# Squares of the last four weight tiles taken in the first step, and the weights' lower parts by VectorE

## What is computed

```python
def attn(x):                                   # x already layer-normed
    kv_latent = x @ W_to_kv.T                  # 128
    c = kv_latent @ W_compress.T               # 64
    ch = layernorm(c) * ln_gamma + ln_beta
    q = rope(ch @ W_q_comp.T); k, v = split(ch @ W_kv_comp.T); k = rope(k)
    o = softmax(causal(q @ k.T / 8)) @ v
    z = o @ W_comp2lat.T
    return z @ W_to_kv + z @ W_out_res.T + b_out_res

def ffn(x):                                    # x already layer-normed
    hidden = silu(x @ W1.T) * (x @ W3.T)       # 2048
    return fwht(hidden) @ W2.T

x = x + attn(layernorm(x))
x = x + ffn(layernorm(x))
```

## Time and profile before

| | us |
|---|---|
| three runs | 2194.49, 2202.16, 2198.07 |
| median | 2198.07 |
| profiled execution | 2193.52 |
| its span, first to last instruction | 2191.7 |
| TensorE busy in the span | 2106.2 |
| VectorE, ScalarE, GpSimd busy | 1435.8, 941.5, 231.3 |
| mean granted TensorE clock | 0.988 |

### The profile page before, as it was taken

The page is one execution under the profiler, slowest core; times in us unless marked ns, Lnnn a source line. Parts: engine busy times, 40 slices in busy tenths (PEclk is TensorE's granted clock), DMA queues, the critical chain, the costliest instruction groups (busy, mean ns, idle before and its releaser), DMA issues. The chain is left out here.

```text
span 2191.7 us, 27021 instructions
## 1 busy us (share of the span) xinstructions
PE 2106.2 (96%) x9884; PEld 986.1 (45%) x9884; DVE 1435.8 (66%) x2758; ACT 941.5 (43%) x1437; POOL 231.3 (11%) x212
## 2 busy tenths in 40 slices
PE   6668999999999999999999999999999999999999
PEld 3433444444444444444444444444444444444444
DVE  7887676766667666765767666775757657663333
ACT  6846555434433534435444444435344444432221
POOL 2354554000000000000000000000000000000000
PEclk8889999999999999999999999999999999999999
DMA  8435324733337333544146333463236432363121
GB/s 326 152 115 198 126 78 132 192 105 132 103 104 176 100 107 111 142 146 140 57 130 167 119 117 106 120 169 120 80 111 167 132 124 75 113 149 119 69 80 75
DMA packets 231141, 278.65 MB, mean 127 GB/s; under 512 B 178016, under 2 KB 178144, under 8 KB 225632
## 3 DMA queue, kind: packets, MB, share of 16 engines
q1 hardware_dynamic: 231008, 276.91, 41.0%
HBM read 194.81 MB, written 39.85 MB: 107 GB/s over the span
## 5 line engine op out<-in xcount | busy, mean ns | idle before, releaser
L845 PE MATMUL PF<-XF,WS 128*128 128x512 f16 x1792 | 683.9, 382 | 16.0 <-DVE PF L1805 11.9
L846 PE MATMUL PF<-XF,WS 128*128 128x512 f16 x1792 | 681.6, 380 | 0.0
L847 PE MATMUL PF<-XF,WS 128*128 128x512 f16 x1792 | 681.3, 380 | 0.0
L869 PE MATMUL PD<-W2S,H 128*128 128x512 f16 x1024 | 388.1, 379 | 0.0
L870 PE MATMUL PD<-W2S,H 128*128 128x512 f16 x1024 | 388.1, 379 | 0.0
L871 PE MATMUL PD<-W2S,H 128*128 128x512 f16 x1024 | 388.1, 379 | 0.0
L1212 ACT ACTIVATE SH<-PF,afs 128x512 f32<-128x512 f32 x256 | 175.9, 687 | 405.6 <-PE PF L847 401.1
L845 PEld LDWEIGHTS PF<-XF,WS 128*128 128x128 f16 x1792 | 175.4, 98 | 254.3 <-issue 37.4
L1827 DVE TENSOR_TENSOR H<-SH,H 128x1024 f16<-128x1024 f32 x128 | 158.9, 1241 | 181.2 <-ACT H L1223 180.9
L847 PEld LDWEIGHTS PF<-XF,WS 128*128 128x128 f16 x1792 | 175.9, 98 | 213.0 <-issue 2.8
L1819 DVE SCALAR_TENSOR_TENSOR SH<-PF,afs,SH 128x512 f32<-128x512 f32 x256 | 191.6, 748 | 117.9 <-ACT SH L1212 105.3
(11 more groups left out here) (317 smaller groups left out, 2086.9 us busy)
## 6 DMA issues: line engine op xcount, KB each, us to landing
WS<-wscr SPq DMA_DIRECT2D x112, 896.0 KB, 4.9
W2S<-w2scr SPq DMA_DIRECT2D x30, 1024.0 KB, 6.5
ring<-x SPq DMA_DIRECT2D x56, 256.0 KB, 7.1
wscr<-WS SPq DMA_DIRECT2D x16, 896.0 KB, 4.0
out<-ring SPq DMA_DIRECT2D x56, 256.0 KB, 2.6
XF<-w SPq DMA_DIRECT2D x16, 512.0 KB, 7.8
RAW<-w13t SPq DMA_DIRECT2D x16, 512.0 KB, 4.0
xraw<-xT SPq DMA_DIRECT2D x28, 256.0 KB, 5.0
```

What stands on the lines that cost most here:

```text
L845: pe.matmul(bank, wh, th, start=i < 2 and j == 0, stop=False, skip_group_check=True)
L846: pe.matmul(bank, wh, tl, start=False, stop=False, skip_group_check=True)
L847: m = pe.matmul(bank, wl, th, start=False, stop=j == 1, skip_group_check=True)
L869: pe.matmul(PD[:, t % 2, :], th, wh, start=j == 0, stop=False)
```

## The change

Two things are changed in step 0 and ahead of it; from step 1 on the lists are the same.

1. The sums of squares of tiles 12 to 15 leave the hand-written part. Their rows are no longer loaded to XF but to the last eight places of the ring (`norm_row`), where the rows of x for chunks 2 and 3 come later; `norm_rows` of these four waits for what R and wsm are last read by, and `load_x` of chunks 2 and 3 waits for all 32 sums instead. ScalarE takes 12, 13 and 14 in tile 0, after the second silu, and 15 in tile 1, ahead of `copy_p5`. `tokens_high(0, i)`, which overwrites XF, waits for 24 sums.
2. All lower parts are VectorE's: `forms_low(h, part)`, part 0 for forms 0 to 3 and part 1 for forms 4 to 6, both counted by v_wl; GpSimd's `forms_low` and g_wl are gone. In a tile, part 0 stands after `fill(k, 2)`, behind `sum_c`, and part 1 behind `sum_e`; before, VectorE's stood ahead of `sum_c`.

With these go moves: `forms_high(h + 1, ...)` from before `fill(k, 0)` and after `copy_p5` to after `fill(k, 1)`; `forms(h + 2)` from j = 2 to j = 5; `store_forms` from j = 3 to j = 5 (6 at h = 10); `scale2` from f = 12 to f = 11, ahead of the attention's piece; `scale_rows` of 3 to 15 one to eight places later.

```diff
-SCALE_AT = dict(zip((1, 5, 12, 20, 26, 32, 38, 45, 55, 62, 68, 76, 83, 92), range(2, NH)))
+SCALE_AT = dict(zip((1, 8, 15, 22, 31, 38, 44, 50, 57, 63, 70, 77, 85, 93), range(2, NH)))
+        def norm_row(h):
+            return rows[:, h % 7, :] if h < 12 else flat[:, 4096 + 1024 * (h - 12):5120 + 1024 * (h - 12)]
...
@@ def load_x(a):
                 elif a == 4:
                     w.wait_ge(a_wh, 2 * NH)
-                    w.wait_ge(g_wl, NH)
-                    w.wait_ge(v_wl, NH)
+                    w.wait_ge(v_wl, 2 * NH)
                     w.wait_ge(p_wb, NH)
                 elif a >= 2:
-                    w.wait_ge(v_bb, 1)
-                    w.wait_ge(v_M, 1)
-                    w.wait_ge(a_m, 4)
+                    w.wait_ge(a_nm, 2 * NH)
...
+                if h >= 12:
+                    w.wait_ge(v_bb, 1)
+                    w.wait_ge(v_M, 1)
+                    w.wait_ge(a_m, 4)
-                sp.dma_start(rows[:, h % 7, :], w13[:, h, :]).then_inc(d_n[h % 7], 16)
+                sp.dma_start(norm_row(h), w13[:, h, :]).then_inc(d_n[h % 7], 16)
...
-                    if s == 0 and j == 3 and 1 <= h < NH - 1:
+                    if s == 0 and j == (6 if h == 10 else 5) and 1 <= h < NH - 1:
                         store_forms(h + 1)
@@ def _(ac):
             trans1(1, 3, 1)
-            norms(12, 0)
             parts_o1(1, 2)
-            norms(12, 1)
-            norms(13, 0)
             parts_o1(1, 3)
-            norms(13, 1)
             xtrans1(0, 0)
-            norms(14, 0)
             xtrans1(0, 1)
-            norms(14, 1)
             xtrans1(0, 2)
-            norms(15, 0)
             xtrans1(0, 3)
-            norms(15, 1)
             tokens_high(0, 0)
...
-                if split:
-                    forms_high(h + 1, 0)
                 fill(k, 0)
+                if k == 1:
+                    norms(15, 0)
+                    norms(15, 1)
                 copy_p5(k)
+                fill(k, 1)
                 if split:
+                    forms_high(h + 1, 0)
                     forms_high(h + 1, 1)
-                fill(k, 1)
                 fill(k, 2)
                 silu(k, 0)
...
                 silu(k, 1)
+                if k == 0:
+                    norms(12, 0)
+                    norms(12, 1)
                 fill(k, 5)
+                if k == 0:
+                    norms(13, 0)
+                    norms(13, 1)
                 if k % 4 < 3:
                     fill(k, 6)
+                if k == 0:
+                    norms(14, 0)
+                    norms(14, 1)
@@ def _(ve):
-            def forms_low(h):
-                w.wait_ge(a_wh, 2 * h + 2)
-                ve.tensor_tensor(WS[:, h % 2, 1, 4:7, :], WF[:, 4:7, :], WS[:, h % 2, 0, 4:7, :], ALU.subtract).then_inc(v_wl, 1)
+            def forms_low(h, part):
+                w.wait_ge(a_wh, 2 * h + part + 1)
+                f = slice(0, 4) if part == 0 else slice(4, 7)
+                ve.tensor_tensor(WS[:, h % 2, 1, f, :], WF[:, f, :], WS[:, h % 2, 0, f, :], ALU.subtract).then_inc(v_wl, 1)
...
+                if s == 0 and f == SUMS_AT + 1:
+                    scale2()
                 if s + 1 < NS:
-                    for c, slot in slots(s, 7 * h + j):
+                    for c, slot in slots(s, f):
                         attention(2 * s + 2 + c, slot)
...
-                    if f == SUMS_AT + 2:
-                        scale2()
...
                 fill(k, 1)
-                if s == 0 and 1 <= h < NH - 1:
-                    forms_low(h + 1)
...
                 fill(k, 2)
+                if s == 0 and 1 <= h < NH - 1:
+                    forms_low(h + 1, 0)
                 fill(k, 3)
                 sum_e(k)
+                if s == 0 and 1 <= h < NH - 1:
+                    forms_low(h + 1, 1)
@@ def _(gp):
-            def forms_low(h):
-                w.wait_ge(a_wh, 2 * h + 1)
-                gp.tensor_tensor(WS[:, h % 2, 1, 0:4, :], WF[:, 0:4, :], WS[:, h % 2, 0, 0:4, :], ALU.subtract).then_inc(g_wl, 1)
...
-                        if j == 0 and 1 <= h < NH - 1:
-                            forms_low(h + 1)
-                        if j == 2 and h < NH - 2:
+                        if j == 5 and h < NH - 2:
                             forms(h + 2)
```

More of the change, by code:

```diff
@@ L376, in build_kernel @@
         g_bias = sem("g_bias")
-        g_dg, g_wm, g_s, g_wl = (sem(f"g_{s}") for s in ("dg", "wm", "s", "wl"))
+        g_dg, g_wm, g_s = (sem(f"g_{s}") for s in ("dg", "wm", "s"))
         block = ctx.enter_context(nc.Block())
@@ L449, in store_forms @@
                 w.wait_ge(a_wh, 2 * h + 2)
-                w.wait_ge(g_wl, h + 1)
-                w.wait_ge(v_wl, h + 1)
+                w.wait_ge(v_wl, 2 * h + 2)
                 sp.dma_start(wscr[h], WS[:, h % 2].rearrange("p a b c -> p (a b c)")).then_inc(d_wst[h % 2], 16)
@@ L827, in product @@
                         w.wait_ge(a_wh, 2 * k + 2)
-                        w.wait_ge(g_wl, k + 1)
-                        w.wait_ge(v_wl, k + 1)
+                        w.wait_ge(v_wl, 2 * k + 2)
                     else:
@@ L1096, in norms @@
                 c = 96 + i * 16 + h
-                r = rows[:, h % 7, i * 512:(i + 1) * 512]
+                r = norm_row(h)[:, i * 512:(i + 1) * 512]
                 ac.activation(r, r, ACT.Square, accum_out=st[:, c:c + 1]).then_inc(a_nm, 1)
@@ L1184, in tokens_high @@
                 if s == 0:
-                    w.wait_ge(a_nm, 2 * NH)
+                    w.wait_ge(a_nm, 24)
                 elif i >= 3:
@@ L1400, in _ @@
                         tokens_high(0, i)
+                fill(k, 0)
+                if k == 1:
+                    norms(15, 0)
+                    norms(15, 1)
+                copy_p5(k)
+                fill(k, 1)
                 if split:
                     forms_high(h + 1, 0)
-                fill(k, 0)
-                copy_p5(k)
-                if split:
                     forms_high(h + 1, 1)
-                fill(k, 1)
                 fill(k, 2)
@@ L1933, in _ @@
             outp1(1, 0)
-            forms_low(0)
+            forms_low(0, 0)
+            forms_low(0, 1)
             max1(1, 2)
@@ L1956, in _ @@
             tokens_low(0, 3)
-            forms_low(1)
+            forms_low(1, 0)
+            forms_low(1, 1)
             tokens_sum(0, 1)
@@ L1967, in fill @@
                 s, h = divmod(k, NH)
+                f = 7 * h + j
+                if s == 0 and f == SUMS_AT + 1:
+                    scale2()
                 if s + 1 < NS:
[L1969 removed]
+                    for c, slot in slots(s, f):
                         attention(2 * s + 2 + c, slot)
[L1971 removed]
                 if s == 0:
@@ L2060, in forms @@
                 w.wait_ge(a_wh, 2 * h)
-                w.wait_ge(v_wl, h)
-                w.wait_ge(g_wl, h)
+                w.wait_ge(v_wl, 2 * h)
                 for i in range(2):
```

1 line of the change is left out of this document (removed).

## The result

The changed kernel takes **2185.01 us** (median of four runs, 2184.20 to 2186.56) against 2198.70 us (median of four, 2194.49 to 2202.16) of the kernel before, run beside it: ratio 0.9939, 95% interval 0.9921 to 0.9958. The forecast was 2183.0 in a range of 2174 to 2197, faster by over 0.3% with a chance of 0.76. It came out so; its sum for the profiled executions did not. Those are 2184.20 us after and 2193.52 before, 9.3 us apart where the sum said 15.1. The two differences, 13.7 between the medians and 9.3 between the traces, are both right, and why they differ is the main thing the experiments found.

The account below looks back on a forecast made before the run. It took TensorE's first-step idle to be waits for VectorE, held up by GpSimd's 128x1024 subtraction. Terms -1.1 - 7.5 + 0 - 7.5 + 1.0 gave -15.1 us: 2178.4 profiled, 2183 median, range 2174 to 2197.

Parts of the forecast that it names:

- rival 4: All that the waits hold is won, no new wait comes, and the half clock goes too: -24, 2174 us; chance 0.05.
- A: Ahead of the products: a lock goes and sums leave ScalarE, so product 1 comes 1.1 us earlier (bounds 0.3 and 2.5).
- B: Tiles 0 to 2: VectorE locks and waits go, `scale2` moves ahead of the statistics; -7.5 us (-3.7 to -9).
- F: Later places of `store_forms`, `load_raw`, `forms` at j 5 and `scale_rows`: no cost.
- C: Tiles 2 and 3: lower parts come back (+1.5), a lock and a `forms_high` go (-1.5); 0 us (-2 to +2).
- D: Tiles 4 to 15: shorter TensorE waits, -10.6, against 3 us more on VectorE; -7.5 us (-13 to +1).
- E: Sums moved to ScalarE in tiles 0 and 1, mostly hidden, with possible table loads: +1.0 us (0 to +2.6).
- Rival 2: Slower: product 0 of the next tile waits for the lower parts, the lateness handed on; 2209.5 us, chance 0.09.
- Rival 1: VectorE becomes the first step's bound, gains returning as waits for `split2`, rope and `sum_e`; about -1 us, 2197, chance 0.15.
- Rival 3: The table loads and late rows of x both land on the path: +5 on the sum, 2188 us; chance 0.07.

Follow-up runs that it names:

- e7: The kernel before, unchanged, run once more for a second trace: 2198.53 us, ratio 1.0000.
- e5: The changed kernel with GpSimd's bias additions at slots 18 and 19 instead of 8 and 9: 2175.78 us, ratio 0.9909.
- e1: The kernel before with only the eight halves of sums of squares moved: 2197.94 us, ratio 1.0007.
- e2: The changed kernel with the sums of squares, and the loads of x that follow them, back in their old places: 2185.06 us, ratio 0.9950.
- e3: The changed kernel with part 0 of the lower parts back on GpSimd, after product 2 (j = 2): 2186.48 us, ratio 0.9955.
- e4: The changed kernel with both lower parts of a tile ahead of `sum_c` on VectorE: 2199.78 us, ratio 1.0013.
- e6: The changed kernel with `scale2` back at f = 12, behind the statistics: 2184.09 us, ratio 0.9946.
- e9: The changed kernel with GpSimd making the forms ahead of the bias at j = 5: 2184.77 us, ratio 0.9938.

## Why the prediction was right, and where it was not

That the median came within 2 us is partly luck: two errors met. The sum put the profiled execution at 2178.4 us, 5.8 below what it was; and to it I added the 4.55 us by which the median had stood above the profiled execution before, as if that were a constant, where it is 0.8 us in the changed kernel. By the table of the first step it is none: the idle time of the first step is 34.8 and 33.7 us in the two traces, the busy time 262.7 and 270.7. Against e7's trace the change is worth 15.6 us (2198.0 to 2182.4): 2.9 ahead of the step, 5.1 of idle and 9.5 of busy time in it, and 1.9 lost after it. Against the first trace it is 9.3: 2.8, 6.3, 1.4 and 1.2 lost. **The idle time won in the first step is 5 to 6 us of some 14**; ahead of it 2.8 are won, and a good part of the rest is TensorE running less at half clock (mean granted clock of the step 0.98, against 0.95 in e7 and 0.97 in the first trace). Over the rows of the table busy time grows from 258 us at a mean clock of 0.99 to 271 at 0.95, for the same matmuls. My forecast had that term in a rival only (rival 4, "the half clock that follows long idle goes with it"), at 0.05; it belonged in the sum. In the kernel before, the matmuls behind the wait of 4.65 us start 0.43 us apart from 159.69 to 161.82, at a clock of 0.50, and 0.22 us apart from 163.02 on. The first step was to come near 284 us and took 289.8.

**A** is exact at its place: product 1 of tile 0 starts at 120.27 us, before 121.37, so 1.10 earlier, as forecast.

```profile
120.27 0.61 PE L849 MATMUL PF<-XF,WS 128*128 128x512 f16 x1 [5.27 <-DVE XF L1795]
```

Product 0 came forward 2.8 us (forecast 2.5). Most of that is given back in this wait, 5.27 us where 2.89 stood, and product 1 keeps 1.1.

**B** said -7.5 from there to product 4 of tile 2, and it was -3.5 (171.46 to 166.86, less A). The front of it came as told: the first W2 product starts at 149.23 us, 9.0 earlier (forecast some 8). The failed step is "the locks at 157.04 and after it (1.9) come from GpSimd's bias additions, which stay: 0 to 1.9". They did not stay at 1.9. In the kernel before, GpSimd's four additions of the bias were over at 159.36 us, before most of the chain of the norm, whose last ten operations then ran at 0.16 us each (rows of that trace, GpSimd's and VectorE's):

```profile
154.43 4.93 POOL L2046 TENSOR_TENSOR ring<-ring,bb 128x512 f32<-128x512 f32 x4
...
161.98 0.15 DVE L1429 TENSOR_TENSOR st<-st 128x4 f32<-128x4 f32 x1
```

In the changed kernel the chain comes earlier and falls beside the bias and, new at j = 5, beside `forms`. It loses 4.9 us in tile 2 (8.9 against the 4.0 of e5), by its rows 2.6 of them beside `forms` and 2.1 beside the bias. Step F had costed `forms` at j = 5 at nothing by looking only at who waits for it, not at whom it holds up. e5 shows the price: without this, tiles 2 and 8 are 11.4 us shorter, the clock's part included.

**C** said 0 and was -1.2 (tile 4 starts 5.83 us earlier, product 4 of tile 2 by 4.60).

**D** said -7.5 for tiles 4 to 15 and was -4.7 (213.1 to 208.4 us). By its own items: the wait for `sum_c` gave 5.7 us (forecast 5.0), the one for line 1458 gave 2.5 (2.0). The two others failed: the wait for the parts of o gave 1.1 (1.8), since ScalarE's part now ends last, and the one for V did not give 1.8 but took 2.1, by the same norm chain, in tile 8. The bound "VectorE has 3 us more, the whole on the path" was about right by luck: 1.9 us of waits for ScalarE's `copy_b` are new. All of D's gain lies in tiles 4 to 7, which went from 73.1 to 67.6 us; tiles 8 to 15 took 140.0 us before and take 140.8 now.

**E** said +1.0 and was about 0: e1 and e2 show no cost that can be told from nothing, and the trace has no table load at that place: the square of 130.48 us follows the silu of 129.91 us with none between them. The loads of x are issued at 139.15 us, forecast 138, and nobody waits for them:

```profile
139.15 1.76 SPq L401 DMA_DIRECT2D ring<-x  x4
```

**F**: the stores and `scale_rows` did cost nothing; `forms`, as told above, did cost something.

**The reason named first was the lesser one.** The forecast argued from VectorE being held up by GpSimd's 128x1024 subtraction, counted at 18 us. Those 18 are gone in the changed kernel, and 10 others came (34.7 to 26.7 in all). e3 has more time held up in all than the kernel before and nearly all of the gain; e4 has less than the changed kernel and none of it. What counts is what stands ahead of the operation for which TensorE waits. The sum did carry this, in D's first item and in B's "no longer stands ahead", so it came out in the right region with the wrong headline.

**The rivals.** Rival 2 is refuted: no wait of product 0 for the lower parts is in the trace of the changed kernel. Rival 1 came in part, as 7.8 us of waits for the split and 3.9 for V, but these did not take up what the others gave. Rival 3 is refuted by E. Rival 4 had the clock right; with e5 its time, 2174, is nearly reached (2175.8), by an edit that is not in the change.

What stays open: how much of the gain is the clock and how much the stall was not set apart by any run, since over the kernels the low clock goes with the stalls (in the changed kernel it is 0.92, 0.93 and 0.85 in tiles 0, 2 and 8, the ones with long stalls left, and in e5 tile 2 and tiles 4 to 15 run at 1.00), though the two stalls of e7 told above had it in one execution and not in the other. The 1.2 to 1.9 us lost behind the first step are mostly one wait of TensorE for a DMA of transposed probabilities in tile 85 (1.7 us). e4, e5, e6 and e9 have it too, e2, e3 and the kernel before don't, and e2 takes the same time as the changed kernel; its cause stays open, and so does the share that the unseparated moves (high parts, `forms`, stores) have in the gain.

## What to carry to other kernels

Work that is wanted only by the next tile belongs behind the operation that the busiest engine waits for, whatever engine does it: here that place was worth 15 us of 2198 with the rest of the change kept, and the engine 1.5. Ask as well what the moved work itself waits for, since its wait is handed on to all that is queued behind it (in e4 7.6 us of waiting for ScalarE, with `sum_c` behind). When stalls are taken away, look again at which instructions of GpSimd now run beside VectorE's chains of small operations: time each chain against GpSimd's row, and move what is not urgent (here the bias, by ten slots, for another 9 us). And before a sum is made against one trace, split its stretches into busy and idle time at the granted clock; here a difference in the busy time of the same matmuls was the clock (262.7 us at 0.97, 270.7 at 0.95, and 258.1 at 0.99 in e5, which has the least idle time, 22.2 us).

## What the runs showed of the hardware

A VectorE operation on 128x4 values of `st` takes 0.16 us alone (e5, 153.93). In the changed kernel, beside GpSimd additions or multiplications of two 128x512 tiles (1.25 us each), such an operation took 1.18 us at 154.42 and 1.19 at 158.73 and 159.95; in e9 three in a row took 1.18, 1.19 and 1.18 (156.57 to 160.20). Beside additions of two 128x256 tiles (0.72 to 0.74 us each) it took 0.57 to 0.70 us (155.83, 158.12, 265.75, 266.45), and in the kernel before, beside a subtraction of 128x1024 (2.12 and 2.13 us), it took 2.03 us at 80.63 and 1.99 at 277.98. In these cases, where the view shows the end of the GpSimd instruction, VectorE's ends 0.01 to 0.03 us after it. Eight of the fifteen operations in tile 2 of the changed kernel are at 0.15 to 0.20 us: four (155.63, 156.32, 157.71, 157.92) start at most 0.16 us from the end of a GpSimd instruction, and four run beside GpSimd's TENSOR_SCALAR on 128x128 values (161.10, 1.18 us for two); in tile 8 one beside these took 0.35 (271.67). The price in these traces is up to one GpSimd instruction for each small VectorE one, so that the chain pays again and again (4.9 us for the fifteen in tile 2, 8.9 against the 4.0 of e5).

The same kernel ran the same 316 matmuls of tiles 4 to 7 in 73.1 and in 77.7 us, with equal idle time and a granted clock of 1.00 and 0.93. I had taken the spread of the kernel before, 9 us over ten executions, for noise of the measurement. In the two traces that there are, it is a different share of the first step at a granted clock of 0.50 (mean 0.97 and 0.95), and the mean clock of 56 executions tends to fall as their time grows, on one chip too (2193.0 us in the middle at 0.986 or more, 2198.5 at 0.983 or less).
